# A decoder layer stack in float32 on one core: where the two value matmuls of a tile stand among the tensor engine's work

## The reference

```python
for i in range(6):
    x = attn_layer(shift_tokens(x), Wqkv[i], q_scale[i], k_scale[i], Wo[i]) + x
    x = ffn_layer(shift_tokens(x), ln_g[i], ln_b[i], W1[i], b1[i], W2[i], b2[i]) + x

# attn_layer: q, k, v = split(x @ Wqkv)            128 -> 3 x 1024, 16 heads of 64
#             q = l2norm(q) * qs;  k = l2norm(k) * ksc;  rotary with tables on both
#             sim = 8 * q k^T in windows of 32, masked;  attn = softmax(sim)
#             out = (attn @ v) @ Wo                 1024 -> 128
# ffn_layer:  xn = layernorm(x) * g + b;  a, gate = split(xn @ W1 + b1)
#             a * gelu(gate) @ W2 + b2              341 inner features
```

## Time and profile before

| | us |
|---|---|
| median of 3 runs (3251.1 to 3257.75) | 3251.88 |
| the profiled execution | 3248.79 |
| its span in the trace | 3246.7 |
| PE busy | 3164.7 |
| DVE busy | 2797.1 |
| ACT busy | 2536.7 |
| POOL busy | 2332.1 |

### The profile page before, as it was taken

One profiled execution on the slowest core, in us unless ns is written; L12 is line 12 of the kernel. 1 busy time (PEld: TensorE's weight loads), 2 busy tenths in 40 slices (PEclk: granted clock), 3 DMA queues, 4 the chain that ended last, 5 costly groups with the idle time before them and its releaser, 6 DMA issues.

```text
span 3246.7 us, 125159 instructions
## 1 busy us (share of the span) xinstructions
PE 3164.7 (97%) x51271; PEld 2479.1 (76%) x51271; DVE 2797.1 (86%) x5489; ACT 2536.7 (78%) x5156; POOL 2332.1 (72%) x3927
## 2 busy tenths in 40 slices
PE   7989998899999999999999999999999999999997
PEld 5677787577777777777777777777777777777776
DVE  6844444899999999999999999999999999999996
ACT  6856665588888888888888888888888888888886
POOL 6722222878777787777887787787788777877784
PEclk9999999999999999999999999999999999999998
DMA  4000000555556655556555565555565555555552
GB/s 109 3 7 8 8 9 13 118 117 109 109 108 124 122 106 106 106 116 124 116 109 109 111 123 118 104 109 106 121 126 111 108 108 113 106 110 108 113 113 59
DMA packets 280546, 310.50 MB, mean 96 GB/s; under 512 B 154281, under 2 KB 225582, under 8 KB 279982
## 3 DMA queue, kind: packets, MB, share of 16 engines
q0 software_dynamic: 58368, 201.36, 33.9%
q1 hardware_dynamic: 220892, 100.93, 12.9%
q10 hardware_dynamic: 722, 0.21, 0.0%
HBM read 23.63 MB, written 2.10 MB: 8 GB/s over the span
## 4 chain that ended last, share of the span: by engine, by line
PE 90%; DVE 2%; POOL 2%; issue 2%; ACT 1%; DMA 1%; SPq 1%; DVEq 0%; POOLq 0%; ACTq 0%
PE bank L1197 11%; PE bank L1257 10%; PE bank L1143 10%; PE bank L1175 10%; PE bank L1231 9%; PE bank L1114 7%; PE bank L1246 6%; PE bank L1216 5%; PE bank L1130 5%; PE bank L1154 3%; PE bank L729 2%; PE bank L1211 2%; PE bank L742 2%; PE bank L751 2%; PE bank L806 2%
## 5 line engine op out<-in xcount | busy, mean ns | idle before, releaser
L1435 DVE TENSOR_TENSOR RK<-bank,tables 128x1024 f32<-128x1024 f32 x384 | 467.9, 1220 | 46.6 <-PE bank L1114 46.3
L1421 DVE TENSOR_TENSOR RQ<-bank,q_tables 128x1024 f32<-128x1024 f32 x384 | 451.7, 1218 | 31.1 <-ACT sq L1316 9.4
L1561 POOL DMA_DIRECT2D RK<-RK x192 | 175.9, 916 | 372.5 <-DVE RK L1435 355.9
L1569 POOL TENSOR_TENSOR RK<-RK,rn 128x512 f32<-128x512 f32 x384 | 401.7, 1046 | 34.2 <-DMA RK<-RK 33.0
L1575 POOL TENSOR_TENSOR P<-P,rn 128x512 f32<-128x512 f32 x384 | 403.8, 1051 | 0.1
L1581 POOL TENSOR_TENSOR P<-P,inv_sum 128x512 f32<-128x512 f32 x384 | 394.2, 1048 | 0.4 <-DVE inv_sum L1506 0.3
L1555 POOL DMA_DIRECT2D RQ<-RQ x384 | 387.6, 1313 | 2.3 <-issue 2.3
L1197 PE MATMUL bank<-WV,xcT 128*128 128x512 f32 x768 | 380.5, 618 | 0.0
L1143 PE MATMUL bank<-xcT,WQ 128*128 128x128 f32 x3072 | 374.9, 275 | 3.9 <-ACT xcT L1289 3.9
L1257 PE MATMUL bank<-WO,OT 128*128 128x128 f32 x3072 | 374.6, 275 | 0.0
L1175 PE MATMUL bank<-WA,xcT 128*128 128x512 f32 x768 | 361.7, 593 | 1.8 <-DVE P L1485 1.8
(11 more groups left out here) (169 smaller groups left out, 7437.6 us busy)
## 6 DMA issues: line engine op xcount, KB each, us to landing
RK<-RK POOLq DMA_DIRECT2D x192, 512.0 KB, 5.1
RQ<-RQ POOLq DMA_DIRECT2D x384, 256.0 KB, 6.7
Z<-Z SPq DMA_DIRECT2D x768, 64.0 KB, 4.6
WA<-in_wqkv SPq DMA_DIRECT2D x24, 256.0 KB, 2.9
ystat<-Y SPq DMA_DIRECT2D x192, 32.0 KB
ystat<-Y SPq DMA_DIRECT2D x384, 15.8 KB
ys<-Y SPq DMA_DIRECT2D x192, 32.0 KB
ys<-Y SPq DMA_DIRECT2D x384, 15.8 KB
```

Of the source, the lines that this page charges most:

```text
L1421: tt(both, src.unsqueeze(1).to_broadcast([128, 2, 8, SEQ]), m.q_tables[:, layer(t), :, :].unsqueeze(2).to_broadcast([128, 2, 8, SEQ]), ALU ...
L1435: tt(both, src.unsqueeze(1).to_broadcast([128, 2, 16, 32]), tab.unsqueeze(2).to_broadcast([128, 2, 16, 32]), ALU.mult).then_inc(s.rotated. ...
L1569: tt(part, part, wide(m.rn[:, t % 4, 16 + 8 * j:24 + 8 * j]), ALU.mult).then_inc(s.k_scaled.sem, 1)
```

## The change

It moves instructions in the lists of all five engines and gives `WV` and `W1` two buffers each; no instruction is added or taken away. Both value matmuls now stand ahead of `head_outputs`, half 0 first and half 1 second, with the transpose of the query lengths between them; `head_outputs` is directly followed by `scores`. The second half of the keys is made after the transposes of the keys, and the second feed-forward matmuls before the query lengths. As the values of tile `i` are now made before `head_outputs(i-4)` has read the same one of the four `V` buffers, `values_out(t, 0)` on ACT waits for the products of tile `t-4`. ACT does both halves of the exponentials ahead of the values. DVE does both key halves in a row, and `query_floor` after them. POOL scales both halves of the keys before both halves of the scores. On SP the input of a coming tile is issued before the feed-forward input instead of behind it.

```diff
-        m.WV = sb("WV", [128, INNER])
+        m.WV = sb("WV", [128, 2, INNER])
-        m.W1 = sb("W1", [128, 2 * FF])
+        m.W1 = sb("W1", [128, 2, 2 * FF])
-        m.trilbd = sb("trilbd", [128, 128])
-        m.trilT = sb("trilT", [128, 128])
+        m.trilbd, m.trilT = m.OT[:, 0, 512:640], m.OT[:, 1, 512:640]
@@ SP, weights
-            if n == 6 and l > 0:
-                sp.wait_ge(s.ff, 3 * first)
-                load_first_ff(sp, m, l)
-                if n == TILES - 1:
-                    sp.wait_ge(s.v.sem, s.v.upto(0, first + TILES))
+                if n == 10:
                     load_value_weights(sp, m, l + 1)
+                if n == 12:
+                    at_least(sp, s.ff, 3 * first)
+                    load_first_ff(sp, m, l + 1)
@@ SP, the loop
-        for i in range(N + LAST + 1):
-            ff_input(i - 5)
+        for i in range(N + LAST + 2):
+            ff_input(i - 6)
+            probs_moved(i - 4)
             layer_input(i + 1)
...
-            probs_moved(i - 3)
@@ PE, values: waits
-                if j == 1:
+                if j == 0:
                     pe.wait_ge(m.w_v, 16 * layer(t) + 16)
+                    at_least(pe, s.k_copied.sem, s.k_copied.upto(0, t))
+                else:
                     at_least(pe, s.xn_copied, t - 5)
@@ PE, the loop
             keys(i, 0)
+            keys_turned(i - 1, 1)
+            ff_out(i - 8)
+            query_lengths(i)
+            keys_turned(i - 1, 0)
             keys(i, 1)
-            keys_turned(i - 1, 1)
-            query_lengths(i)
-            ff_out(i - 8)
-            keys_turned(i - 1, 0)
+            normal_turned(i - 6)
+            values(i, 0)
             query_lengths_turned(i)
-            normal_turned(i - 6)
+            values(i, 1)
             head_outputs(i - 4)
-            values(i, 1)
-            values(i, 0)
             scores(i - 1)
             ff_in(i - 7)
@@ ACT, values_out
+                if bb == 0:
+                    at_least(act, s.o, 2 * (t - 3))
@@ ACT, the loop
+            squares(i, KEYS, 0)
             normalised(i - 6)
             keys_out(i - 1, 1)
+            keys_out(i - 1, 0)
+            query_lengths_out(i)
+            normal_out(i - 6)
             squares(i, KEYS, 1)
...
             exponents(i - 2, 1)
-            values_out(i, 1)
+            exponents(i - 2, 0)
+            values_out(i, 0)
             outputs_out(i - 4, 1)
-            values_out(i, 0)
             outputs_out(i - 4, 0)
             seeded(i)
-            exponents(i - 2, 0)
+            values_out(i, 1)
@@ DVE, the loop
+            key_rotary(i, 0)
             key_rotary(i, 1)
             query_floor(i)
-            key_rotary(i, 0)
...
+            row_sums(i - 2, 1)
             maximum(i - 1, 1)
             maximum(i - 1, 0)
-            less_maximum(i - 1, 0)
-            row_sums(i - 2, 1)
+            row_sums(i - 2, 0)
+            attention_added(i - 4)
             less_maximum(i - 1, 1)
             inverse_sums(i - 2, 1)
-            attention_added(i - 4)
             gated(i - 7)
-            row_sums(i - 2, 0)
+            less_maximum(i - 1, 0)
             inverse_sums(i - 2, 0)
@@ POOL, the loop
+            keys_scaled(i, 1)
             mean_shift(i - 5)
-            keys_scaled(i, 1)
+            keys_scaled(i, 0)
             scores_scaled(i - 1, 0)
-            keys_scaled(i, 0)
             scores_scaled(i - 1, 1)
```

More of the change, by code:

```diff
@@ L336, in load_value_weights @@
 def load_value_weights(sp, m, l):
-    sp.dma_start(m.WV[:, :], m.wqkv[l, :, 2 * INNER:3 * INNER]).then_inc(m.w_v, 16)
+    sp.dma_start(m.WV[:, l % 2, :], m.wqkv[l, :, 2 * INNER:3 * INNER]).then_inc(m.w_v, 16)
 def load_output_weights(sp, m, l, par):
@@ L347, in load_first_ff @@
 def load_first_ff(sp, m, l):
-    sp.dma_start(m.W1[:, :], m.w1[l, :, :]).then_inc(m.w_1, 16)
+    sp.dma_start(m.W1[:, l % 2, :], m.w1[l, :, :]).then_inc(m.w_1, 16)
 def load_second_ff(sp, m, l, par):
@@ L1009, in local @@
     s.x_turned, s.x_copied = sem("local_x_turned"), sem("local_x_copied")
-    s.qk, s.squared, s.rotated = counted("qk", *four), counted("squared", (QUERIES, 0), (QUERIES, 1), (KEYS, 1), (KEYS, 0)), counted("rotated", (QUERIES, 0), (QUERIES, 1), (KEYS, 1), (KEYS, 0))
+    s.qk, s.squared, s.rotated = counted("qk", *four), counted("squared", *four), counted("rotated", *four)
     s.summed, s.k_floor = sem("local_summed"), sem("local_k_floor")
@@ L1017, in local @@
     s.k_turned, s.k_copied = counted("k_turned", 1, 0), counted("k_copied", 1, 0)
-    s.v, s.v_copied = counted("v", 1, 0), counted("v_copied", 1, 0)
-    s.scores, s.mx, s.less = sem("local_scores"), counted("mx", 1, 0), counted("less", 0, 1)
+    s.v, s.v_copied = counted("v", 0, 1), counted("v_copied", 0, 1)
+    s.scores, s.mx, s.less = sem("local_scores"), counted("mx", 1, 0), counted("less", 1, 0)
     s.scaled, s.probs, s.row_sum = counted("scaled", 0, 1), counted("probs", 1, 0), counted("row_sum", 1, 0)
@@ L1081, in weights @@
             first = l * TILES
-            if n == 6 and l > 0:
-                sp.wait_ge(s.ff, 3 * first)
-                load_first_ff(sp, m, l)
             if l + 1 < DEPTH:
                 if 2 <= n < 6:
-                    at_least(sp, s.v.sem, s.v.upto(0, first))
+                    at_least(sp, s.v.sem, s.v.upto(1, first))
                     load_input_weights(sp, m, l + 1, (l + 1) % 2, n - 2)
@@ L1194, in values @@
                         pe.wait_ge(s.rotated.sem, s.rotated.upto((QUERIES, 1), t + 1))
-                else:
-                    at_least(pe, s.k_copied.sem, s.k_copied.upto(0, t))
-                mm(V_BANK[j][:, :], m.xsT[:, t % 2, :], m.WV[:, j * 512:(j + 1) * 512], start=True, stop=True)\
+                mm(V_BANK[j][:, :], m.xsT[:, t % 2, :], m.WV[:, layer(t) % 2, j * 512:(j + 1) * 512], start=True, stop=True)\
                     .then_inc(s.v.sem, 1)
@@ L1206, in scores @@
                 if t == N - 1:
-                    pe.wait_ge(s.less.sem, s.less.upto(1, t))
+                    pe.wait_ge(s.less.sem, s.less.upto(0, t))
                 crossed = ((0, 0), (1, 1), (0, 1), (1, 0))
@@ L1230, in ff_in @@
                     for side, off in ((0, FF), (1, 0)):
-                        last = mm(FF_BANK[c][0:rows, side * 128:(side + 1) * 128], m.W1[:, off + at:off + at + rows],
+                        last = mm(FF_BANK[c][0:rows, side * 128:(side + 1) * 128], m.W1[:, layer(t) % 2, off + at:off + at + rows],
                                   m.xnT[:, t % 2, :], start=True, stop=True)
@@ L1318, in squares @@
                 else:
-                    if half == 1:
+                    if half == 0:
                         at_least(act, s.summed, t)
@@ L1374, in _ @@
             squares(i, QUERIES, 1)
+            squares(i, KEYS, 0)
+            if i == 0:
+                m.cross_tail()
             normalised(i - 6)
             keys_out(i - 1, 1)
+            keys_out(i - 1, 0)
+            query_lengths_out(i)
+            normal_out(i - 6)
             squares(i, KEYS, 1)
-            if i == 0:
-                m.cross_tail()
-            query_lengths_out(i)
-            squares(i, KEYS, 0)
-            normal_out(i - 6)
-            keys_out(i - 1, 0)
             exponents(i - 2, 1)
-            values_out(i, 1)
+            exponents(i - 2, 0)
+            values_out(i, 0)
             outputs_out(i - 4, 1)
-            values_out(i, 0)
             outputs_out(i - 4, 0)
             seeded(i)
-            exponents(i - 2, 0)
+            values_out(i, 1)
             if i % TILES == 20 and i + TILES < N:
```

10 lines of the change are left out of this document (5 added, 5 removed).

## The result

The change made the kernel faster: 3198.05 us in the median (3192.96 to 3203.0, 4 runs) against 3251.49 (3244.05 to 3257.75, 4 runs), a ratio of 0.9838 [0.9822, 0.9854]. The profiled execution took 3192.96 us, its span 3190.9, against 3248.79 and 3246.7. The forecast was 3196.

The account below looks back on a forecast made before the run. PE was taken as the bound (90% of the chain of waits). 3248.79 - 57 (shapes) + 4 (POOL) - 4 (SP) = 3192 profiled; 3195 as median, plus 1 for the tightest wait: 3196, range 3186 to 3210.

Parts of the forecast that it names:

- tile shapes: On PE, one way out of and one way into the 64x64 tiles go, saving 0.31 us a turn.
- the unknown hand-over: On PE, from the float32 products to the bf16 mask: between 0.05 and 0.15 us, taken as 0.05.
- the wait for the keys' copy: Values half 0 wait for ACT's copy of the keys' half 0: 0.06 us of room, cost taken as 0.
- the way out of the query lengths: On PE, ahead of the keys' transposes of half 0: 0.10 us, making that group 0.54.
- Positions: PE's new turn, placed from old distances: each group's start after the turn's start, next turn at +13.43 us.
- DVE's wait ahead of the last rotary: DVE, ready at about +8.5, waits half a microsecond for ACT's squares of the second key half, until +9.02.
- POOL: Keys' transposes, half 1, wait for POOL's scaling behind its transfer: room falls from 1.7 to 0.7 us; +4 us net.
- slower rival: Keys' transposes wait for POOL every turn, its transfer landing beyond 6.5 us: 3265 or, at 6.8, 3307 us; chance 0.07.
- SP, `Z` and the buffers: PE's 3.9 us of waits for `Z` go, and second `WV` and `W1` buffers free a blocked SP: together -4 us.
- The 57 us for the shapes: Total saving on PE from fewer changes of tile shape: 184 turns x 0.31 us.

Follow-up runs that it names:

- e1: The changed kernel with value half 1 put back between the products and the scores: 3250.25 us, ratio 0.9995.
- e8: The changed kernel with the query lengths transposed ahead of both value halves and copied by ACT ahead of the keys' half 0: 3215.13 us.
- e2: The changed kernel with the second feed-forward matmuls ahead of the transposes of the keys' half 1: 3199.89 us.
- e7: The changed kernel with SP's old list and one buffer each for WV and W1: 3200.03 us.
- e4: The changed kernel, SP's new list kept, with one buffer each for WV and W1, loaded where the kernel before loads them: 3272.19 us.
- e5: The changed kernel with 32 more transposes (64 instructions) on PE, once, in turn 3: 3211.35 us.
- e3: The kernel before with only the values moved ahead of the products, ACT's first value copy waiting for its buffer: 3512.03 us, ratio 1.0808.
- e9: The kernel of e8 with 8 more transposes (16 instructions) on PE, once, in turn 3: 3199.08 us.

## Why the prediction was right

- **The saving a turn, step "tile shapes".** Predicted 0.31, measured 0.317, and e1 gives it back as 0.320 with nothing else changed. The choice of the low bound for the unknown hand-over (0.05 of 0.05 to 0.15) was right; it is 0.03. The weighing against the Trainium skill stands too: 128 cycles of drain (the Trainium skill, TensorE: Matmul & The Clock Gate, Step-by-step) would be an estimated 0.11 us for the two changes. The rows and e1 say 0.32.
- **One term was mis-sized: the wait for the keys' copy.** Priced at 0 to 0.05, taken as 0. From the start of half 0 of the values to the next group it is 0.906 us, where the two matmuls of a key half take 0.861, and e8, which removes the wait, shows 13.420 - 13.374 = 0.046 a turn, some 8 us. That the turn came out at 13.42 in spite of it is because another term was too dear: the way out of the query lengths, counted at 0.10 in front of the transposes of half 0, is 0.05 (0.493 for the group where 0.54 was forecast). The two errors cancel, by luck. The argument that durations on ACT vary by a few ns was also too strong: the copies of the keys before took 586 to 628 ns.
- **Positions.** The second key half was forecast at +6.87 and is at +6.81, the products at +9.76 and 9.75, the mask at +10.74 and 10.73, the next turn at +13.43 and 13.42. DVE's wait ahead of the last rotary, "half a microsecond" at +9.02, is 0.47 at +8.96. So the moved pieces cost nothing beyond the 0.046 above.
- **POOL.** Taken as +4 us net. The step's own terms, 8 less the 6.3 already lost, give 1.7, and the 6.3 was misread: it is what the weight loads waited, and PE's distances at these transposes show 0.7 us of it before. They show 2.0 us after, so the change added 1.3; e2 shows that giving POOL more room brings nothing to be seen. The waits behind the transfer became more (95 against 54). The slower rival needed a landing of over 6.5 us in every turn; one of 192 transfers took that long (6.6 us). The median landing went from 5.1 to 5.4 us. The sharing of the DMA engines that speaks for this rival (the Trainium skill, Trainium Kernel Development and Optimization, Key Constraints) agrees in direction with that, but the queries' transfers and those of `Z` landed sooner than before (6.6 against 6.7 us, 4.1 against 4.6), and no run shows that sharing made the 0.3 us.
- **SP, `Z` and the buffers, -4 us.** The products' wait for `Z` is gone; PE's distances show 2.3 us of it before, not 3.9. With it went 2.6 us that the prediction had not counted, waits ahead of the mask in the last turns. Not right was that the second buffers take anything away: e7 has one of each and is as fast. The step read a wait of SP as a cost without asking what is queued behind it. What it missed is the other side, that with the new list of SP the single buffers would have cost 74 us (e4).
- **Not foreseen at all: 5.0 us of standstills in the scores**, which the trace of before has nowhere. They, 2.2 us between the queries and the keys in six turns, where PE waits for DVE to empty the bank that the keys use (the view below is for 640 to 3116 us), and 1.85 us between the products and the mask are most of why the standstills doubled from 5.9 to 12.5 us, where +4 and -4 were reckoned. The delays ahead of the mask are some 0.04 us each in turns with remainder 2 by four, from turn 10 on. In e5 they stand in turns with remainder 3, so they too go with the place of the code; how they come about is open. The 6.6 us were mostly made good by the three edges outside these turns (4.4 us) and by 0.317 a turn instead of 0.31, which is luck: the sum had no terms for either.

```profile
PE bank L1173 <- DVE P L1485: 1.4, 4, 0.6
```

- **The time.** 3192 for the profiled execution against 3192.96 measured; 3196 against a median of 3198.05. The 57 us for the shapes were right for the stated reason. That the total is met to 2 us, when runs of the changed kernel differ by 10, is partly the luck of the small terms.

## What to carry to other kernels

Where PE bounds and its groups use different tile shapes, put groups of one shape next to each other: here each pair of changes costs 0.32 us, with both value halves between (before) as with one (e1), and it is read from starts, not from durations or idle times. Such a move pays only if the other engines' lists are moved with it (e3: 8% slower for the same order on PE), so work out for each new neighbour what it waits for. Of a transfer that may be held at its queue, ask what stands behind it before its buffer is called too small.

## What the runs showed of the hardware that was not expected

- PE can stand still for up to 1.6 us amid a run of independent matmuls, behind one fixed instruction, in turns four apart, where 16 KB of its instructions (about 256) end. It goes on 1.2 to 1.6 us after a load on the instruction queue is done. Shifting the code by 8, 28 or 32 matmuls moved the place by exactly as many. Over the whole stage the scores lost between 0 and 35 us to it. The same loop with 16 instructions more ahead of it (e9 against e8) is 16 us faster, 0.5%; and e8 has the shortest turn of all, 13.374 us, and is 17 us slower than the change.
- A change between 128x128 and 64x64 tiles costs 0.09 to 0.11 us at the change, and the way back costs a second 0.10 in the next float32 matmul of 512 columns; between float32 and bf16 on the same 64x64 tiles it costs nothing to be seen (0.03 us from start to start).
